# Node work of three graph convolutions moved into the visits of their neighbour sums

## What is computed

```python
def _gcn_conv(x, src, dst, norm, W, b, n_nodes):
    h = x @ W
    msg = h[src] * norm[:, None]
    out = jax.ops.segment_sum(msg, dst, num_segments=n_nodes)
    return out + b
...
h = jax.nn.relu(_gcn_conv(x, src, dst, norm, W1, b1, n))
h = jax.nn.relu(_gcn_conv(h, src, dst, norm, W2, b2, n))
h = jax.nn.relu(_gcn_conv(h, src, dst, norm, W3, b3, n))
...
h = jnp.maximum(_layernorm(x, axis=-1), 0.0)
q = (x @ Wq).reshape(N, N_HEADS, D_HEAD)
k = (x @ Wk).reshape(N, N_HEADS, D_HEAD)
v = (x @ Wv).reshape(N, N_HEADS, D_HEAD)
```

## Time and profile before

| | us |
|---|---|
| median of three runs | 16398.22 |
| the profiled execution: its own time | 16390.01 |
| its span | 16388.3 |
| POOL busy | 10536.2 |
| PE busy | 7263.1 |
| DVE busy | 5726.5 |
| ACT busy | 2889.0 |

### The profile page before, as it was taken

The page is one execution under the profiler, slowest core; times in us unless marked ns, Lnnn a source line. Parts: engine busy times, 40 slices in busy tenths (PEclk is TensorE's granted clock), DMA queues, the critical chain, the costliest instruction groups (busy, mean ns, idle before and its releaser), DMA issues. The chain is left out here.

```text
span 16388.3 us, 210648 instructions
## 1 busy us (share of the span) xinstructions
PE 7263.1 (44%) x43306; PEld 5194.0 (32%) x43356; DVE 5726.5 (35%) x10642; ACT 2889.0 (18%) x3659; POOL 10536.2 (64%) x10566
## 2 busy tenths in 40 slices
PE   2311111233333111115555535558889867455556
PEld 1111111122222111114444423335555536333435
DVE  4511113111113111121111147767777742323332
ACT  1111111455551111110000000012222211000001
POOL 0377774677772777767777743346666652777774
PEclk8655555677675555555555555579999975777676
DMA  4111111322221111112222212211111112111112
GB/s 145 19 19 19 19 19 36 85 77 77 77 77 26 19 19 19 19 15 52 49 49 49 49 32 67 67 31 33 33 33 33 33 40 58 21 21 21 21 21 48
DMA packets 652644, 675.65 MB, mean 41 GB/s; under 512 B 303477, under 2 KB 489790, under 8 KB 649663
## 3 DMA queue, kind: packets, MB, share of 16 engines
q0 software_dynamic: 340624, 383.65, 12.6%
q1 hardware_dynamic: 280958, 278.52, 5.6%
q10 hardware_dynamic: 30384, 7.79, 0.3%
HBM read 517.39 MB, written 149.11 MB: 41 GB/s over the span
## 5 line engine op out<-in xcount | busy, mean ns | idle before, releaser
L884 POOL DMA_INDIRECT gcn_sum_ring<-scratch_parts,gcn_sum_staged x4704 | 4684.5, 996 | 1961.9 <-issue 1395.6
L979 PE MATMUL gcn_sum_totals<-gcn_sum_rows,gcn_sum_onehot 128*128 128x98 bf16 (+2 forms) x9408 | 1290.0, 319 | 5113.9 <-ACT gcn_sum_rows L945 5107.2
L979 PEld LDWEIGHTS gcn_sum_totals<-gcn_sum_rows,gcn_sum_onehot 128*128 128x128 bf16 x9408 | 973.0, 158 | 5431.5 <-issue 5365.5
L865 DVE TENSOR_TENSOR gcn_sum_onehot<-k_columns,k_group_rel 128x2048 bf16<-128x2048 bf16 x594 | 728.5, 1227 | 5041.1 <-PE gcn_sum_totals L979 4863.1
L703 POOL DMA_INDIRECT sh_ring<-scratch_tab,sh_staged x1664 | 1879.4, 1129 | 830.1 <-issue 506.9
L703 POOL DMA_INDIRECT rel_ring<-scratch_tab,rel_staged x1664 | 1702.4, 1023 | 832.5 <-issue 476.1
L945 ACT COPY gcn_sum_rows<-gcn_sum_ring 128x1536 bf16 (+1 forms) x588 | 1604.6, 2751 | 2924.3 <-SPq L897 2916.4
L1339 POOL DMA_INDIRECT score_ring<-scratch_tab,score_staged x1664 | 1737.5, 1044 | 533.2 <-issue 506.8
L642 PE MATMUL sh_accumulator<-sh_message,sh_onehot 128*128 128x248 f32 x3328 | 1209.7, 543 | 1245.6 <-DVE sh_message L2002 1242.4
L642 PE MATMUL rel_accumulator<-rel_message,rel_onehot 128*128 128x512 f32 x3328 | 1609.3, 628 | 2.8 <-ACT rel_accumulator L675 2.8
L642 PEld LDWEIGHTS sh_accumulator<-sh_message,sh_onehot 128*128 128x128 f32 x3328 | 950.6, 293 | 1504.1 <-issue 1326.4
(11 more groups left out here) (393 smaller groups left out, 9375.7 us busy)
## 6 DMA issues: line engine op xcount, KB each, us to landing
gcn_sum_ring<-scratch_parts,gcn_sum_staged POOLq DMA_INDIRECT x4704
scratch_kv<-score_ring SPq DMA_DIRECT2D x208, 256.0 KB, 2.0
value_ring<-scratch_kv SPq DMA_DIRECT2D x208, 256.0 KB, 2.6
rel_ring<-scratch_tab,rel_staged POOLq DMA_INDIRECT x1672
score_ring<-scratch_tab,score_staged POOLq DMA_INDIRECT x1664, 2.5
sh_ring<-scratch_tab,sh_staged POOLq DMA_INDIRECT x1664, 2.4
scratch_totals<-rel_taken SPq DMA_DIRECT2D x102, 256.0 KB
rlo_lin_chunk<-scratch_totals SPq DMA_DIRECT2D x98, 256.0 KB, 2.9
```

The source lines that it names most:

```text
L865: return nc.vector.tensor_tensor(out[:], k["columns"][:], k["group_rel"][:, bass.ds(step * GT, GT)].unsqueeze(1).to_broadcast([P, P, GT]), ...
L884: nc.gpsimd.indirect_dma_start(out=ring[:, q % slots, g, :], out_offset=None, in_=table, in_offset=bass.IndirectOffsetOnAxis(ap=staged[:, ...
L979: done = nc.tensor.matmul(totals[:, q, 0:held], onehot[q % 2][:, :, g], rows[q % 2][:, g, :], start=(g == 0), stop=(g == GT - 1))
```

## The change

The three calls of `group_sums` become `first_sums`, `second_sums` and `third_sums`. Each still goes through the 196 pairs, with the same gathers, `rows` copies and 16 matmuls. New is what one visit does behind the multiply, spread over the next visits by lags, so that each engine's queue holds pieces of several pairs:

- The sum of a tile is kept in two small tiles. `keep` says whether the pair goes on with the tile of the pair before; the sum is multiplied by it and the new part added. A tile that is visited twice has its node work done twice, and the second result overwrites the first.
- First sum: the own row and `dinv`, a transpose on PE, a copy by ACT, the layer on PE, relu and scale on ACT (twice), the split into three parts on DVE, and the store into the next table from ACT's queue. The bias rides as a row of ones.
- Second sum: the same with W2, then a second transpose and W3.
- Third sum: own row, bias, relu, residual, and the norm of `x` by small DVE steps and a root on ACT, then q k v on PE; k and v are stored to `tab64`, q stays in SBUF.
- The one-hot is [edge partition, 16 steps, 128 columns], f32 `iota` against bf16 `group_rel`; the bf16 tile `columns` is kept in `group_tables` only.
- PE's `totals` have two banks in place of four. Pairs 0 to 7 and the last few are written out; the rest is a loop over four.
- `step_tables` stands behind the convolutions instead of ahead of them.

The diff, cut to its core:

```diff
-def _group_one_hot(nc, k, out, step):
-
-    return nc.vector.tensor_tensor(out[:], k["columns"][:],
-                                   k["group_rel"][:, bass.ds(step * GT, GT)].unsqueeze(1).to_broadcast([P, P, GT]), ALU.is_equal)
...
-        node_linear(nc, k, "gcn_lin1", sums[:].rearrange("p j f -> p (j f)"), JP // 4, 1, w1, wide[:].rearrange("p j f -> p (j f)"))
-        store_parts(nc, "gcn_parts1", dram["parts128"], wide, HID)
-        store_table(nc, "gcn_table1", dram["tab128"], wide, HID)
-            node_linear(nc, k, "gcn_lin2", flat, J, 1, w2, flat)
-            node_linear(nc, k, "gcn_lin3", flat, J, 1, w3, h[:].rearrange("p j f -> p (j f)"))
-            store_parts(nc, "gcn_parts2", dram["parts32"], h, D)
...
+BASE, AHEAD = 16, 8
...
+def _pairs(engine, body, lag):
+    for n in range(AHEAD):
+        body(n, n % 4)
+    with engine.Fori(0, (NS - AHEAD) // 4) as i:
+        for q in range(4):
+            body(i * 4 + q + AHEAD, q)
+    for n in range(NS, NS + lag):
+        body(n, n % 4)
...
+def _pair_one_hot(nc, k, out, n):
+    return nc.vector.tensor_tensor(out[:], k["iota"][:].unsqueeze(1).to_broadcast([P, GT, P]),
+                                   k["group_rel"][:, bass.ds(n * GT, GT)].unsqueeze(2).to_broadcast([P, GT, P]), ALU.is_equal)
...
+    def copy_rows(self, act, k, m, q, marks=None):
+        need = _word_of(act, k, W_NEED, m, 1, NG)
+        slot = _word_of(act, k, W_SLOT, m, 0, 1)
+        act.wait_ge(self.landed, need)
+        act.wait_ge(self.multiplied, m - 1 + BASE)
+        if marks is not None:
+            self.nc.scalar.copy(self.rows[q % 2][:, :, 3 * self.width:self.held], marks[:, bass.ds(need * GT, GT), :])
+        self.nc.scalar.copy(self.rows[q % 2][:, :, 0:3 * self.width],
+                            self.ring[:, bass.ds(slot, 1), :, :].rearrange("p o g w -> p (o g) w")).then_inc(self.copied, 1)
+    def make_one_hot(self, dve, k, m, q):
+        dve.wait_ge(self.multiplied, m - 1 + BASE)
+        _pair_one_hot(self.nc, k, self.onehot[q % 2], m).then_inc(self.made, 1)
+    def multiply(self, pe, m, q):
+        pe.wait_ge(self.folded, m - 1 + BASE)
+        pe.wait_ge(self.made, m + 1)
+        pe.wait_ge(self.copied, m + 1 + BASE)
+        for g in range(GT):
+            last = self.nc.tensor.matmul(self.totals[:, q % 2, 0:self.held], self.onehot[q % 2][:, g, :], self.rows[q % 2][:, g, :],
+                                         start=(g == 0), stop=(g == GT - 1))
+        last.then_inc(self.multiplied, 1)
+    def fold(self, dve, k, m, q):
+        dve.wait_ge(self.multiplied, m + 1 + BASE)
+        self.nc.vector.tensor_reduce(self.joined[q % 2][:], self.totals[:, q % 2, 0:3 * self.width].rearrange("p (c f) -> p f c", c=3),
+                                     axis=AX_X, op=ALU.add).then_inc(self.folding, 1)
+        dve.wait_ge(self.folding, m + 1)
+        self.nc.vector.scalar_tensor_tensor(out=self.sums[q % 2][:], in0=self.sums[(q + 1) % 2][:], scalar=k["keep"][:, bass.ds(m, 1)],
+                                            in1=self.joined[q % 2][:], op0=ALU.mult, op1=ALU.add).then_inc(self.folded, 1)
+        dve.wait_ge(self.folded, m + 1 + BASE)
+    def begin(self, dve):
+        self.nc.vector.memset(self.sums[1][:], 0.0)
+        dve.sem_inc(self.folded, BASE)
...
+def second_sums(nc, k, dram, wide, w2, b2, w3, own):
...
+        def add_own(dve, m, q):
+            tile = _tile_of(dve, k, m)
+            got.fold(dve, k, m, q)
+            _linked(dve, scaling, m + 1, nc.vector.tensor_tensor(held[q % 2][:], got.sums[q % 2][:], _tile(wide, tile), ALU.add))
+            dve.wait_ge(flipped, m - 1 + BASE)
+            nc.vector.tensor_scalar(scaled[q % 2][:], held[q % 2][:], k["dinv"][:, bass.ds(tile, 1)], None, ALU.mult).then_inc(summed, 1)
+        def split_rows(dve, m, q):
+            tile = _tile_of(dve, k, m)
+            high, middle, low = (parts[q][:, c * D:(c + 1) * D] for c in range(3))
+            dve.wait_ge(stored, (m - 3 + BASE) * DMA)
+            dve.wait_ge(narrowed, m + 1)
+            nc.vector.tensor_copy(_tile(own, tile), narrow_ps[:, 0:D])
+            _linked(dve, splitting, 3 * m + 1, nc.vector.tensor_copy(high, narrow_ps[:, 0:D]))
+            _linked(dve, splitting, 3 * m + 2, nc.vector.tensor_tensor(rest[q % 2][:], narrow_ps[:, 0:D], high, ALU.subtract))
+            _linked(dve, splitting, 3 * m + 3, nc.vector.tensor_copy(middle, rest[q % 2][:]))
+            nc.vector.tensor_tensor(low, rest[q % 2][:], middle, ALU.subtract).then_inc(split, 1)
...
+                def body(n, q):
+                    if _live(n, 0):
+                        got.copy_rows(act, k, n, q)
+                    if _live(n, 2):
+                        turn(act, n - 2, (q + 2) % 4)
+                    if _live(n, 3):
+                        activate(act, n - 3, (q + 1) % 4)
+                    if _live(n, 4):
+                        turn_again(act, n - 4, q)
+                    if _live(n, 7):
+                        store(act, n - 7, (q + 1) % 4)
+                _pairs(act, body, 7)
...
+def third_sums(nc, k, dram, own, b3, w, x_next, q_nodes):
...
+        def add_own(dve, m, q):
+            tile = _tile_of(dve, k, m)
+            a, b, c = (w_[q % 2][:] for w_ in work)
+            got.fold(dve, k, m, q)
+            at = m * 8
+            _linked(dve, steps, at + 1, nc.vector.tensor_tensor(a, got.sums[q % 2][:], _tile(own, tile), ALU.add))
+            _linked(dve, steps, at + 2, nc.vector.scalar_tensor_tensor(out=b, in0=a, scalar=k["dinv"][:, bass.ds(tile, 1)], in1=b3[:],
+                                                                       op0=ALU.mult, op1=ALU.add))
+            _linked(dve, steps, at + 3, nc.vector.scalar_tensor_tensor(out=moved[q % 2][:], in0=b, scalar=0.0, in1=_tile(k["x"], tile),
+                                                                       op0=ALU.max, op1=ALU.add))
+            _linked(dve, steps, at + 4, nc.vector.tensor_reduce(mean[q % 2][:, 0:1], moved[q % 2][:], axis=AX_X, op=ALU.add))
+            _linked(dve, steps, at + 5, nc.vector.tensor_single_scalar(mean[q % 2][:, 1:2], mean[q % 2][:, 0:1], 1.0 / D, op=ALU.mult))
+            _linked(dve, steps, at + 6, nc.vector.tensor_scalar(centered[q % 2][:], moved[q % 2][:], mean[q % 2][:, 1:2], None, ALU.subtract))
+            _linked(dve, steps, at + 7, nc.vector.tensor_tensor(c, centered[q % 2][:], centered[q % 2][:], ALU.mult))
+            _linked(dve, steps, at + 8, nc.vector.tensor_reduce(var[q][:, 0:1], c, axis=AX_X, op=ALU.add))
+            nc.vector.tensor_scalar(var[q][:, 1:2], var[q][:, 0:1], 1.0 / D, 1e-5, ALU.mult, ALU.add).then_inc(varied, 1)
...
+        def normalize(dve, m, q):
+            tile = _tile_of(dve, k, m)
+            dve.wait_ge(rooted, m + 1)
+            _linked(dve, norming, 2 * m + 1, nc.vector.reciprocal(root[q % 2][:, 1:2], root[q % 2][:, 0:1]))
+            dve.wait_ge(flipped, m - 1 + BASE)
+            _linked(dve, norming, 2 * m + 2, nc.vector.tensor_scalar(normal[q % 2][:], centered[q % 2][:], root[q % 2][:, 1:2], 0.0, ALU.mult, ALU.max))
+            nc.vector.tensor_tensor(_tile(x_next, tile), moved[q % 2][:], normal[q % 2][:], ALU.add).then_inc(normed, 1)
...
+                got.begin(dve)
+                dve.sem_inc(normed, BASE)
+                dve.sem_inc(picked, BASE)
+
+                def body(n, q):
+                    if _live(n, 0):
+                        got.make_one_hot(dve, k, n, q)
+                    if _live(n, 2):
+                        normalize(dve, n - 2, (q + 2) % 4)
+                    if _live(n, 1):
+                        add_own(dve, n - 1, (q + 3) % 4)
+                    if _live(n, 4):
+                        take_query(dve, n - 4, q)
+                _pairs(dve, body, 4)
...
-        norm_relu(nc, k, "att_norm", h)
-        on_vector(nc, "att_add_h", [lambda: v.tensor_tensor(k["x"][:], k["x"][:], h[:], ALU.add)])
-            node_linear(nc, k, "qkv_lin", flat_h, JP // 4, 1, w, qkv[:].rearrange("p j f -> p (j f)"))
-            store_table(nc, "qkv_table", dram["tab64"], qkv[:, :, D:3 * D], 2 * D)
...
-        step_tables(nc, k, dram)
...
+            gcn(nc, io, k, dram, k["x_next"], k["q"])
+        k["x"] = k["x_next"]
...
+        step_tables(nc, k, dram)
+        attention(nc, io, k, dram, k["q"])
```

More of the change, by code:

```diff
@@ L1238, in gcn, with _live, _word_of @@
-def gcn(nc, io, k, dram):
+BASE, AHEAD = 16, 8
+def _live(n, lag):
+    return not isinstance(n, int) or 0 <= n - lag < NS
+def _pairs(engine, body, lag):
[6 more added lines that the diff above has]
+        body(n, n % 4)
+def _word_of(engine, k, row, n, low, high):
+    return engine.value_load(k["group_words"][0:1, row, bass.ds(n, 1)], min_val=low, max_val=high)
@@ L1296, in _ahead @@
+        third_sums(nc, k, dram, own, b3, w, x_next, q_nodes)
 def _ahead(engine, semaphores):
@@ L1811, in _ @@
             def _(pool):
-                _gather_rows(nc, pool, dram["tab64"], staged, ring, indexed, released, gathered,
```

(1 more changed line is left out.)

594 lines of the change are left out of this document (399 added, 195 removed).

## The result

The changed kernel takes 16437.01 us (median of 20 runs, 16408.6 to 16461.3), against 16398.43 us for the kernel before (20 runs beside it): 1.0023 of the time, 95% interval 1.0016 to 1.003. Forecast were 16580 us, so the sign was right and the size four to five times too large: +39 us instead of +182 against the medians, +50 instead of +190 between the two profiled executions. The prediction took 33 us as what can be told from no change; +39 is just above it.

What follows compares the result with a forecast made beforehand. POOL's gathers in the three sums were taken as the bound. From 16390 us, minus 515 for gaps, plus 670 for longer one-hots and 35 for small DVE instructions, gave 16580 us, 1.1% slower; range 16340 to 16840.

Steps and rivals of the forecast that it cites:

- What bounds the kernel: Three neighbour sums: POOL's gathers bound them, other engines have room; about 241 us of POOL time is waiting on DVE one-hots.
- Saved: 515 us: Gaps between the sums: node work leaves them, 654 less 134 of remaining drain and 5 of weight loads.
- 2048 take L = 2.29 us: New one-hot's length L for 2048 elements, from rows with f32 against bf16 operands; the old one took 1.227 us.
- The product of 8000.18 has one operand in PSUM: Attention scores: the gather beside this DVE product takes 0.94 us, so two operands in SBUF decide, not type.
- the formula: A one-hot of length L starting s us into a gather's cycle costs s + L - 1.38 us, never below nothing.
- Added: 670 us: Three sums: 588 longer one-hots stretch gathers by 1.55 us each, 911 us, less the 241 of the old ones.
- Small DVE instructions, 35 us: Each visit's some five short two-SBUF-input instructions also hold gathers, each costing l/2 when meeting a grab; 0 to 90 us.
- Queues that must keep up: DVE (9.6 us per third-sum visit), ACT and PE cost nothing while POOL's group stays the longest.
- Rival 2: Third sum: DVE becomes the bound from 11.6 us a visit; at 13 us the kernel takes 16855 us; chance 0.08.
- Rival 1: One-hots: an f32 operand ends the block, no gather is stretched, 15634 to 15670 us; chance 0.10.
- Rival 4: Gaps: the visits don't hide, each gap keeps 100 us of drain, 16750 us; chance 0.04.
- Rival 3: Sums: gathers and one-hots fall well together, 1.15 us per one-hot, 16345 us; chance 0.16.

Runs made afterwards that it cites:

- experiment 1: The kernel before with only the new one-hot form, nothing of the fusion: 17058.64 us, 1.0402 of before; 1.0142 on a slower chip.
- experiment 3: The changed kernel with the one-hot's iota operand read from a PSUM bank: 15627.22 us, 0.9532 of before; 1.0193 and 1.018 on slower chips.
- experiment 8: The changed kernel, unaltered, run on a slower chip: 19298.69 us beside 19247.53 for the kernel before, 1.0012.
- experiment 2: The changed kernel with the old one-hot form put back: 15869.9 us, 0.9677 of before; 1.0244 on a slower chip.
- experiment 4: The changed kernel with iota in bf16, same new layout: 16432.04 us, 1.0018 of before; 1.0042 on a slower chip.

## Why the prediction was right in sign and wrong in size

- **What bounds the kernel**: right. On chips like that of the comparison, stretching removed or added came out one for one: 576 us of gathers against 582 in the sums, 658 against 661 in experiment 1, 809 against 810 in experiment 3. On the slower chips it did not (experiment 8).
- **"Saved: 515 us"**: right, 529 in the traces, 527 by experiment 2. The second and third gap came out within 4 us of the forecast, the first 12 under it.
- **"2048 take L = 2.29 us"**: right in number, by a reason that was not needed. The layout alone gives it (experiment 4).
- **"The product of 8000.18 has one operand in PSUM"**: right in what it concluded, but that row could not tell. A product of 0.42 us, 0.09 into its gather, costs nothing by the formula wherever its operands lie. The same trace would have told: 31 of the 208 products stand across a gather's start so that the formula gives 0.13 to 0.25 us, and each of these gathers takes 0.940 to 0.947.
- **"Added: 670 us"**, the step that failed: it measured 576. The mechanism was right, the size per one-hot was not. The 1.55 us for a one-hot are right in before's loops (1.53) and too high in the fused ones, where the one-hots start at other places in the gathers' cycle: with 0.944 us for a gather, the sums of 1750.1, 1742.8 and 1768.0 us give 1.38, 1.34 and 1.47 us per visit. I had placed the first sum's at 1.5 and 1.9, the second's at 1.2 and 1.5, and "can't place" the third. Only the second sum's placing was good. Of the 140 us by which the forecast was off between the profiled executions, 670 - 576 = 94 are this term, 35 the next one and 14 the gaps; the rest of the account takes 3 back.
- **Small DVE instructions, 35 us**: some 6 in the changed kernel's trace, and at most 11 in experiment 3's. The price of l/2 does not follow from the prediction's own formula: a start at most 1.20 us into the cycle gives l - 0.18 at the most, 0.01 us for an instruction of 0.19 us and 0.11 for one of 0.29. The 31 of 0.29 us that held a gather in the first sum cost 0.076 each.
- **Queues that must keep up**: right, and with more room than thought. Two folds of the third sum that follow each other directly:

```profile
6001.44 0.26 DVE L1219 TENSOR_REDUCE sum2g_joined<-sum2g_totals 128x32 f32<-128x96 f32 x1 [0.77 <-PE sum2g_totals L1212]
...
6005.37 0.19 DVE L1619 COPY k_q<-sum_linear_ps 128x32 f32 x1 [0.71 <-issue]
6005.53 2.36 DVE L1124 TENSOR_TENSOR sum2g_onehot<-k_iota,k_group_rel 128x2048 bf16<-128x2048 f32 x1
6007.81 0.15 DVE L1586 RECIPROCAL sum_root<-sum_root 128x1 f32<-128x1 f32 x1
...
6009.21 0.26 DVE L1219 TENSOR_REDUCE sum2g_joined<-sum2g_totals 128x32 f32<-128x96 f32 x1 [0.63 <-issue]
```

  This visit takes 7.8 us, not 9.6. Of its three value loads two stand in the open (0.71 and 0.63 us of idle time); the third runs while the one-hot executes and costs nothing. The small instructions take 4.1 us with the pauses between them, where 5.1 were forecast. Rival 2 was far off.
- **Rival 1** (an f32 operand ends the block) is refuted by the gathers of 3.07 us, and experiment 4 shows that type has no part. **Rival 4** (the visits don't hide) is refuted by the gaps. **Rival 3** (they fall well together) had the right mechanism with too large a size: 1.40 us, between its 1.15 and my 1.55. With the terms as measured, "no change" lay at (528.8 + 243.9) / 588 = 1.31 us per one-hot, so the verdict hung on a tenth of a microsecond of starting point.

The measured time lies in the range of 16340 to 16840, near its lower end. What the account leaves is a first-order term whose size depended on six placings, and the middle was taken where each of them was unknown. That the sign came out right, by 39 us, is luck as much as reckoning.

## What to carry to other kernels

Where indirect DMAs on POOL bound a stage, look in its trace for DVE instructions with two SBUF operands beside them, and price each by its own length and start, not DVE's busy share: 402 us of added DVE work with a PSUM source cost 75 us, 628 us of longer one-hots cost 576. Two operands are not the only case: twelve f32 to bf16 casts of the first sum, from SBUF to SBUF with one operand, lengthened a gather too, to at most 1.00 us, as the formula has it. Put one operand in PSUM, or cut the instruction in pieces: the fusion with the old one-hot gave 0.968 of before, these gave 0.953 and 0.972. On the two slower chips all three lost about 2%, so measure on more than one chip. And test a change of form apart from a change of structure: here a gain of 527 us and a loss of 571 had been tied together.
